# The end of a fused attention and mixture-of-experts kernel: roots in smaller slots, two adds on GpSimd, the last batch centred before it is scaled

## The chip, the cores and the metric

One NeuronCore of a Trainium2 chip runs the kernel. The metric is the device time of one execution in microseconds (us). Engines are named as the profile names them: PE is TensorE's matmul side, DVE is VectorE, ACT is ScalarE, POOL is GpSimd, SP is SyncE, and SPq is SP's queue of issued transfers.

## The reference, cut to what matters

Eight batches of 512 tokens with 128 features go through two residual blocks. The first is a small recurrence between two linear layers, the second a top-2 mixture of eight experts. Each block's result is normalised over the features and then added to its input:

```
x = x + _layernorm(_L0_attn_ref(_layernorm(x, axis=-1), ...), axis=-1)
x = x + _layernorm(_L0_ffn_ref(_layernorm(x, axis=-1), ...), axis=-1)
```

with `_layernorm(x) = (x - mean(x)) / sqrt(var(x) + eps)`. The change touches only the last line's outer normalisation and its add, for batches 3, 4, 5 and 7. All is float32.

## The kernel before, in words

Tokens lie on the 128 partitions. A batch has G = 4 groups of 128 tokens, so a batch of x or of sums is a tile of 128 partitions by 512 columns, and one token group is 128 by 128.

The expert stage takes 71 tiles of up to 128 (token, expert) pairs, one per slot of a software pipeline. PE does the three layers (L1593, L1630), ACT writes a tile's weighted result to SBUF (`take_y`, L618), and POOL scatters it to the table `pair_rows` in HBM with an indirect transfer four slots later in program order (`send_y`, L446). In slot t POOL sends tile t - 4. As soon as all tiles of a batch have been sent, SP loads the batch's pairs back (L342 for whole batches; L348 for the two halves of batch 7, which need the last tile).

For each batch DVE then adds the two expert results of a token (`sum_pairs`, L1267; `sum_half`, L1279), takes the statistics (`bn_stats`, L1273 and L1284) and aggregates them to mean and variance (L1291). POOL turns variances to 1/sd (`one_over_sd`: an add of eps at L465, a power of -0.5 at L469), and DVE makes -mean/sd of it (`offset`, L1297). The tuple SD_GROUPS says which batches go together: (0,1), (2,3), (4,5), 6, and 7, the last of which takes ACT's square root (`root_last`, L644) and DVE's reciprocal (L1312) instead of POOL's power. ACT scales and shifts batches 0 to 4 and the first half of 7 (`normalise4`, L636; `normalise_last`, L650). DVE does 5, 6 and the second half of 7 (L1305). DVE adds the result to x for every batch (`add`, L1315, one instruction of 128x512; `add_last`, L1327, two of 128x256).

The order on each engine is written out by hand. DVE after the pipeline: normalise 5, add 5, add 2, offset of 6, normalise 6, add 6, add 3, add 4, the two halves of 7 with their statistics, then 7's root, scaling and add. POOL after the pipeline: only 1/sd of batch 6. SP issues its transfers in one fixed order, each behind its wait. Its end is this:

```
            load_half(0)
            load_half(1)
            sp.wait_ge(s_half_in[1], 16)
            sp.wait_ge(d["out"], 5)
            write_out(3)
            sp.wait_ge(d["out"], 6)
            write_out(1)
            sp.wait_ge(d["out"], 7)
            write_out(2)
            sp.wait_ge(d["out_end"], 1)
            write_half(1)
            sp.wait_ge(d["out_end"], 2)
            write_half(0)
```

`write_out(g)` writes GROUPS[g] of x: group 3 is batch 6 (256 KB), group 1 is batches 2 and 3, group 2 is batches 4 and 5 (512 KB each). A half of batch 7 has 128 KB. `d["out"]` counts DVE's adds in their order on DVE, so that 5 means that batch 6 is added.

Of the kernel before, what the change touches and what calls it, by code (L numbers as in the profile page):

```python
# [13 lines left out]
P = 128  # L14
# [3 lines left out]
G = S // P  # L18
# [35 lines left out]
ROOT2, ROOT3 = 3, 3  # L54

GROUPS = ((0, 2), (2, 4), (4, 6), (6, 7), (7, 8))
SD_GROUPS = ((0, 2), (2, 4), (4, 6), (6, 7), (7, 8))


def sandwich_kernel(nc, x_in, w_in_in, b_in_in, w_out_in, b_out_in, decay_in, mix_in,  # L60
                    gate_in, w0_in, w1_in, wo_in, out):
    ctx = ExitStack()
    with ctx:
# [122 lines left out]
        def half_of_pairs(b, k):  # L186
            return pairs_in[b].rearrange("p (j k d) -> p j k d", k=K, d=D)[:, :, k, :]
# [43 lines left out]
        s_rows_in = [sem(f"tile_in{n}") for n in range(RING)]  # L231
        s_y_sent = [sem(f"y_sent{n}") for n in range(Y_SLOTS)]

        names_d = "out_end m stats mv sd rs nm normed normed_here normed_end out x1"
        d = {n: sem("d_" + n) for n in names_d.split()}
        s_pairs_in = [sem(f"pairs_in{n}") for n in range(len(GROUPS))]
        s_half_in = [sem(f"half_in{n}") for n in range(2)]
# [24 lines left out]
        def sums(n):  # L262

            return half_of_pairs(n // G, 0)[:, n % G, :]
# [15 lines left out]
        def _(sp):  # L280
# [91 lines left out]
            sp.wait_ge(s_half_in[1], 16)  # L372
            sp.wait_ge(d["out"], 5)
            write_out(3)
            sp.wait_ge(d["out"], 6)
            write_out(1)
            sp.wait_ge(d["out"], 7)
            write_out(2)
            sp.wait_ge(d["out_end"], 1)
            write_half(1)  # L380
# [5 lines left out]
        def _(pool):  # L386
# [76 lines left out]
            def one_over_sd(g, first, end):  # L463
                pool.wait_ge(d["mv"], end)
                pool.tensor_tensor(  # L465
                    sd4[:, first * G:end * G], mv4[:, first * G:end * G, 1],
                    eps[:].broadcast_to([P, (end - first) * G]), ALU.add).then_inc(d["sd"], 1)
                pool.wait_ge(d["sd"], g + 1)
                pool.tensor_tensor(  # L469
                    rs4[:, first * G:end * G], sd4[:, first * G:end * G],  # L470
                    minus_half[:].broadcast_to([P, (end - first) * G]),
                    ALU.pow).then_inc(d["rs"], 1)
# [6 lines left out]
            for k, s, t in slots():  # L479
                if t == STEP + 1:  # L480
                    rest_power()
                a_slot(k, s)
                send_y(t - 4)
                if t == FIRST_OLD_TILES + 9:
                    one_over_sd(0, *SD_GROUPS[0])
                elif t == FIRST_OLD_TILES + 11:
                    one_over_sd(1, *SD_GROUPS[1])
                elif t == FIRST_OLD_TILES + 13:
                    one_over_sd(2, *SD_GROUPS[2])

            one_over_sd(3, *SD_GROUPS[3])

        @block.scalar
        def _(act):
# [149 lines left out]
                act.activation(sd4[:, last], mv4[:, last, 1], ACT.Sqrt,  # L644
                               bias=eps[:]).then_inc(d["sd"], 1)

            def normalise_last():
                act.wait_ge(d["nm"], len(SD_GROUPS))
                for n in range((B - 1) * G, (B - 1) * G + G // 2):
                    last = act.activation(sums(n), sums(n), ACT.Identity,  # L650
                                          scale=rs4[:, n:n + 1], bias=nm4[:, n:n + 1])
                last.then_inc(d["normed_end"], 1)


            root(1, 0, mv1, sd1)
            normalise1(0, 0, G)
# [54 lines left out]
            normalise4(2, 4, 0, G)  # L711
            act.activation(unused[:], eps[:], ACT.Sqrt)
            root_last()
            normalise_last()

        @block.vector
        def _(dve):
# [552 lines left out]
            def stats_of(b):  # L1270
                dve.wait_ge(d["m"], b + 1)
                for n in range(b * G, (b + 1) * G):
                    last = dve.bn_stats(stats4[:, n, :], sums(n))  # L1273
                last.then_inc(d["stats"], 1)
# [13 lines left out]
            def aggregate(b):  # L1288
                dve.wait_ge(d["stats"], b + 1)
                for n in range(b * G, (b + 1) * G):  # L1290
                    last = dve.bn_aggr(mv4[:, n, :], stats4[:, n, :])  # L1291
                last.then_inc(d["mv"], 1)

            def offset(g):
                first, end = SD_GROUPS[g]
                dve.wait_ge(d["rs"], g + 1)
                dve.scalar_tensor_tensor(out=nm4[:, first * G:end * G],  # L1297
                                         in0=mv4[:, first * G:end * G, 0], scalar=-1.0,
                                         in1=rs4[:, first * G:end * G], op0=ALU.mult,
                                         op1=ALU.mult).then_inc(d["nm"], 1)  # L1300

            def normalise4(g, b, first, end):
                dve.wait_ge(d["nm"], g + 1)
                for n in range(b * G + first, b * G + end):
                    last = dve.tensor_scalar(sums(n), sums(n), rs4[:, n:n + 1], nm4[:, n:n + 1],  # L1305
                                             ALU.mult, ALU.add)
                last.then_inc(d["normed_here"], 1)

            def one_over_last():
                last = slice((B - 1) * G, B * G)  # L1310
                dve.wait_ge(d["sd"], len(SD_GROUPS))
                dve.reciprocal(rs4[:, last], sd4[:, last]).then_inc(d["rs"], 1)  # L1312
# [5 lines left out]
            def add_normed(b):  # L1318
                dve.wait_ge(d["normed"], b + 1)
                add(b)  # L1320

            def add_here(b):
                dve.wait_ge(d["normed_here"], b - 4)
                add(b)

            def add_last(j):
                return dve.tensor_tensor(  # L1327
                    x[:, (B - 1) * G + j:(B - 1) * G + j + 2],
                    x[:, (B - 1) * G + j:(B - 1) * G + j + 2],
                    half_of_pairs(B - 1, 0)[:, j:j + 2], ALU.add)  # L1330

            def table_start(p):
                full_tiles(p)
# [72 lines left out]
            for k, s, t in slots():  # L1406
                if t == 2:
                    table_start(1)
                elif t == 3:
                    table_end(1)  # L1410
                elif t == 4:
                    use_tiles(1)
                    table_start(2)
                elif t == 5:
                    table_end(2)
                elif t == 6:
                    use_tiles(2)
                if k in ROUNDS:
                    a_slot(k, s, 0)
                chunk_of(t + 1)  # L1420
                times_gate_curve(t - 1)
                fetch_w1(t + 1)
                pairs_of_tiles(t)
                if k in ROUNDS:
                    a_slot(k, s, 1)
                if t == STEP - 2:
                    rest_sums(0, G)
                elif t == STEP - 1:
                    rest_sums(G, 2 * G)
                elif t == STEP:  # L1430
                    rest_mean_var()
                elif t == STEP + 4:
                    rest_offset()
                if FULL_TILES - 5 <= t < FULL_TILES - 5 + B:
                    add_nm2(t - (FULL_TILES - 5))
                if t == FIRST_OLD_TILES + 6:
                    sum_pairs(0, 0)
                    stats_of(0)
                elif t == FIRST_OLD_TILES + 7:
                    aggregate(0)  # L1440
                    sum_pairs(0, 1)
                    stats_of(1)
                elif t == FIRST_OLD_TILES + 8:
                    aggregate(1)
                    sum_pairs(1, 2)
                    stats_of(2)
                elif t == FIRST_OLD_TILES + 9:
                    aggregate(2)
                    sum_pairs(1, 3)
                    stats_of(3)  # L1450
                elif t == FIRST_OLD_TILES + 10:
                    offset(0)
                    aggregate(3)
                    sum_pairs(2, 4)
                    stats_of(4)
                elif t == FIRST_OLD_TILES + 11:
                    aggregate(4)
                    sum_pairs(2, 5)
                    stats_of(5)
                elif t == FIRST_OLD_TILES + 12:  # L1460
                    offset(1)
                    aggregate(5)
                elif t == FIRST_OLD_TILES + 13:
                    sum_pairs(3, 6)
                    stats_of(6)
                elif t == FIRST_OLD_TILES + 14:
                    offset(2)
                    aggregate(6)
                elif t == FIRST_OLD_TILES + 15:
                    add_normed(0)  # L1470
                elif t == FIRST_OLD_TILES + 16:
                    add_normed(1)

            normalise4(2, 5, 0, G)
            add_here(5)
            add_normed(2)
            offset(3)
            normalise4(3, 6, 0, G)
            add_here(6)
            add_normed(3)  # L1480
            add_normed(4)
            sum_half(0)
            stats_of_half(0)
            sum_half(1)
            stats_of_half(1)
            aggregate(7)
            one_over_last()
            offset(4)
            normalise4(4, 7, G // 2, G)
            dve.wait_ge(d["normed_here"], 3)  # L1490
            add_last(G // 2).then_inc(d["out_end"], 1)
            dve.wait_ge(d["normed_end"], 1)
            add_last(0).then_inc(d["out_end"], 1)

        @block.tensor
        def _(pe):
# [207 lines left out]
```

## Time and profile before

| | |
|---|---|
| Time, median of 3 runs | 299.33 us |
| Runs | 299.3 to 300.03 us |
| Span of the profiled execution | 297.5 us |
| The profiled execution's own time | not listed apart; the median less the span is 1.8 us |
| PE busy | 254.9 us (86%) |
| DVE busy | 209.0 us (70%) |
| ACT busy | 176.1 us (59%) |
| POOL busy | 164.7 us (55%) |
| Mean granted TensorE clock | 0.925 |

The span runs from the first to the last instruction. Busy shares are means over the whole program. Only the last 15 us or so matter for this change, and there PE has no work from 282.8 us on.

### The profile page before, as it was taken

The numbers are of one execution on the slowest core, as the hardware profiler recorded it, in microseconds if no ns is written. First come the engines' busy times: TensorE is split into PE (matmuls) and PEld (weight loads), VectorE is DVE, ScalarE is ACT, GpSimd is POOL, SyncE is SP. The second block draws the span as 40 slices with busy tenths as digits, with TensorE's granted clock in tenths as the row PEclk, the third lists the DMA queues.
The fourth block names the chain that finished last, engine by engine and source line by source line (L and its number), as shares of the span: only waits on it lengthen the run. The fifth ranks groups of instructions, "written<-read, shape, count | busy, mean of one in ns | idle before, by whom it ended". The sixth has DMA issues, their size and how long they took to land.

```text
span 297.5 us, 8014 instructions
## 1 busy us (share of the span) xinstructions
PE 254.9 (86%) x2056; PEld 235.2 (79%) x2056; DVE 209.0 (70%) x939; ACT 176.1 (59%) x439; POOL 164.7 (55%) x187
## 2 busy tenths in 40 slices
PE   0667696899988899999999999999999999999900
PEld 0226353799987899899979998999999999999900
DVE  3786989786884587658766956787664444798875
ACT  3634358475665676766674565656566566567681
POOL 8000377784188747874776577577533333247840
PEclk9965559599999999999999999999999999999985
DMA  5899711312310132112212211333333114802047
GB/s 144 181 384 316 209 56 48 81 55 67 74 37 30 52 79 62 45 55 76 64 36 75 75 46 47 98 104 90 92 77 90 43 55 134 334 20 81 19 141 212
DMA packets 28139, 29.65 MB, mean 100 GB/s; under 512 B 4570, under 2 KB 21180, under 8 KB 28096
## 3 DMA queue, kind: packets, MB, share of 16 engines
q1 hardware_dynamic: 22832, 20.04, 23.7%
q0 software_dynamic: 4544, 8.97, 9.4%
q8 instruction: 19, 0.31, 0.5%
q10 hardware_dynamic: 720, 0.13, 0.3%
q14 instruction: 24, 0.20, 0.2%
HBM read 17.53 MB, written 12.05 MB: 99 GB/s over the span
## 4 chain that ended last, share of the span: by engine, by line
PE 54%; DVE 16%; POOL 10%; issue 8%; ACT 7%; DVEq 2%; DMA 1%; ACTq 1%; POOLq 0%
PE bank L1593 28%; PE bank L1630 14%; POOL expert_rows L433 5%; PE bank L1528 3%; PE bank L1544 3%; PE bank L1537 2%; DVE sb_w_now L1236 2%; PE bank L1588 2%; POOL pair_rows L446 2%; POOL sb_rs L414 1%; DVE sb_early L824 1%; DVEq L1230 1%; DMA sb_x<-in_L_attn_x 1%; ACT sb_row L546 1%; ACT sb_early L518 1%
## 5 line engine op out<-in xcount | busy, mean ns | idle before, releaser
L1593 PE MATMUL bank<-sb_xeT,sb_w_now 128*128 128x128 f32 x1136 | 140.9, 277 | 1.9 <-DVE sb_gated L1217 1.9
L1593 PEld LDWEIGHTS bank<-sb_xeT,sb_w_now 128*128 128x128 f32 x1136 | 134.6, 194 | 3.6 <-issue 3.6
L446 POOL DMA_INDIRECT pair_rows<-sb_y_rows,sb_y_pair x71 | 71.3, 1004 | 55.4 <-ACT sb_y_rows L618 38.2
L433 POOL DMA_INDIRECT expert_rows<-sb_row,sb_place x64 | 65.0, 1016 | 47.9 <-DVE sb_place L931 29.0
L1217 DVE TENSOR_TENSOR sb_gated<-bank,sb_silu 128x512 f32<-128x512 f32 x71 | 49.0, 689 | 50.9 <-PE bank L1593 35.7
L1630 PE MATMUL bank<-sb_w_raw,sb_gated 128*128 x568 | 76.2, 277 | 2.2 <-ACT sb_y_rows L618 1.4
L1630 PEld LDWEIGHTS bank<-sb_w_raw,sb_gated 128*128 128x128 f32 x568 | 69.0, 192 | 3.8 <-issue 3.6
L589 ACT ACTIVATE sb_silu<-bank 128x512 f32<-128x512 f32 x71 | 42.5, 598 | 18.0 <-PE bank L1593 15.7
L584 ACT ACTIVATE sb_xeT<-bank 128x128 f32<-128x128 f32 x71 | 19.6, 277 | 56.1 <-PE bank L1588 56.0
L607 ACT ACTIVATE sb_w_now<-sb_w_raw 128x512 f32 x71 | 44.4, 625 | 0.4 <-issue 0.4
L1236 DVE COPY sb_w_now<-sb_w_raw 128x512 f32 x71 | 32.3, 455 | 1.5 <-issue 1.5
L618 ACT ACTIVATE sb_y_rows<-bank,sb_y_weight 128x128 f32<-128x128 f32 x71 | 25.8, 364 | 11.0 <-DVE sb_y_weight L1262 9.1
L1588 PE MATMUL bank<-sb_ident,sb_taken_rows 128*128 128x128 f32 x71 | 19.9, 280 | 0.9 <-DMA sb_taken_rows<-expert_rows 0.9
L546 ACT ACTIVATE sb_row<-sb_x,sb_nm,sb_rs 128x128 f32<-128x128 f32 x32 | 13.7, 485 | 5.1 <-DVE sb_nm L780 5.0
L1528 PEld LDWEIGHTS bank<-sb_w_outT,sb_early 128*128 128x128 f32 x64 | 9.7, 226 | 7.8 <-DVE sb_early L824 7.7
L1528 PE MATMUL bank<-sb_w_outT,sb_early 128*128 128x128 f32 x64 | 10.7, 319 | 5.9 <-DVE sb_early L824 5.9
L1516 PE MATMUL bank<-sb_early,sb_w_inT 128*128 128x512 f32 x16 | 11.1, 783 | 2.5 <-DVE sb_early L816 2.5
L1588 PEld LDWEIGHTS bank<-sb_ident,sb_taken_rows 128*128 128x128 f32 x71 | 10.6, 150 | 2.8 <-DMA sb_taken_rows<-expert_rows 1.0
L1544 PEld LDWEIGHTS bank<-sb_gate,sb_early 128*128 128x128 f32 x64 | 9.4, 226 | 3.1 <-ACT sb_early L553 3.1
L1544 PE MATMUL bank<-sb_gate,sb_early 128*128 128x8 f32 x64 | 9.6, 277 | 2.1 <-ACT sb_early L553 2.1
L411 POOL TENSOR_TENSOR sb_sd<-sb_mv,sb_eps 128x4 f32<-128x4 f32 x10 | 2.1, 208 | 16.6 <-DVE sb_mv L767 16.5
L518 ACT ACTIVATE sb_early<-sb_x,sb_nm,sb_rs 128x128 f32<-128x128 f32 x24 | 10.1, 482 | 2.0 <-DVE sb_nm L780 2.0
(179 smaller groups left out, 276.3 us busy)
## 6 DMA issues: line engine op xcount, KB each, us to landing
sb_taken_rows<-expert_rows SPq DMA_DIRECT2D x71, 65.5 KB, 1.9
sb_w_raw<-in_L_ffn_w SPq DMA_DIRECT2D x2, 2048.0 KB, 14.7
sb_pairs_early<-pair_rows SPq DMA_DIRECT2D x3, 1024.0 KB, 7.2
out_dram<-sb_x SPq DMA_DIRECT2D x3, 512.0 KB, 3.8
pair_rows<-sb_y_rows,sb_y_pair POOLq DMA_INDIRECT x71, 2.3
sb_x<-in_L_attn_x SPq DMA_DIRECT2D x4, 256.0 KB, 5.9
expert_rows<-sb_row,sb_place POOLq DMA_INDIRECT x64, 2.5
expert_rows<-sb_pad_row SPq DMA_DIRECT2D x8, 65.5 KB
```

The source lines that it names most:

```text
L433: pool.indirect_dma_start(expert_rows[:, :], bass.IndirectOffsetOnAxis(ap=place[b % ROWS][:, k, j:j + 1], axis=0), row[b % ROWS][:, j, :], ...
L446: pool.indirect_dma_start(pair_rows[:, :], bass.IndirectOffsetOnAxis(ap=y_pair[group % 2][:, t % PAIRS:t % PAIRS + 1], axis=0), y_rows[slo ...
L589: act.activation(silu[t % 2][:], p_l1[:], ACT.Silu).then_inc(c["silu"], 1)
L607: act.activation(w0_now[t % 2][:].rearrange("p (c f) -> p c f", f=D), w_raw_chunks[:, bass.ds(chunks[t], FC), :], ACT.Copy).then_inc(c["w0 ...
L618: act.activation(y_rows[t % Y_SLOTS][:], p_y[t % 2][:, 0:D], ACT.Copy, scale=y_weight[group % 2][:, t % PAIRS:t % PAIRS + 1]).then_inc(c[" ...
L1217: dve.tensor_tensor(gated[t % 2][:], p_l2[:], silu[t % 2][:], ALU.mult).then_inc(c["gated"], 1)
L1236: dve.tensor_copy(w1_now[t % 2][:].rearrange("p (c f) -> p c f", f=D), w_raw_chunks[:, bass.ds(chunks[t] + W_CHUNKS, FC), :]).then_inc(c[" ...
L1528: last = pe.matmul(p_first(b)[:, j * D:(j + 1) * D], states[b % 2][:, j * P:(j + 1) * P], w_outT[:], start=False, stop=(j == G - 1))
L1544: last = pe.matmul(p_second(b)[:, j * E:(j + 1) * E], xn2T[b % 2][:, j * P:(j + 1) * P], gate[:], start=True, stop=True)
L1588: pe.transpose(p_xeT[:, 0:P], taken_rows[:, t % RING, 0:D], ident[:]).then_inc(c["xeT_ps"], 1)
L1593: last = pe.matmul(to[:, n * P:(n + 1) * P], w[:, n * P:(n + 1) * P], x, start=True, stop=True)
L1630: last = pe.matmul(p_y[t % 2][:, 0:D], gated[t % 2][:, n * P:(n + 1) * P], wo.rearrange("p o d -> p (o d)"), start=(n == 0), stop=(n == FC ...
```

## The change

It does five things. (1) SD_GROUPS has six entries: POOL takes batch 4's roots in slot FIRST_OLD_TILES + 12 and batch 5's in slot + 13, where it took both in slot + 13. (2) DVE's offsets of batches 4 and 5 are two instructions, in slots + 13 and + 14, instead of one in slot + 14. (3) The adds to x of batches 3 and 4 go from DVE to POOL, behind the power of batch 6, and SP waits for them by a semaphore of their own, `added`. (4) For batch 7 the mean is subtracted while ACT takes the root: two groups on POOL in one 128x256 instruction, two on DVE. (5) The last step of batch 7 is then, for each group, one DVE instruction x = sums * (1/sd) + x, four in all. `normalise_last` on ACT, the last offset, the last `normalise4` and the 128x256 adds on DVE are gone.

```diff
-SD_GROUPS = ((0, 2), (2, 4), (4, 6), (6, 7), (7, 8))
+SD_GROUPS = ((0, 2), (2, 4), (4, 5), (5, 6), (6, 7), (7, 8))
...
@@ sync
             write_out(3)
-            sp.wait_ge(d["out"], 6)
+            sp.wait_ge(d["added"], 1)
             write_out(1)
-            sp.wait_ge(d["out"], 7)
+            sp.wait_ge(d["added"], 2)
             write_out(2)
...
@@ gpsimd
                     one_over_sd(1, *SD_GROUPS[1])
+                elif t == FIRST_OLD_TILES + 12:
+                    one_over_sd(2, *SD_GROUPS[2])
                 elif t == FIRST_OLD_TILES + 13:
-                    one_over_sd(2, *SD_GROUPS[2])
-
-            one_over_sd(3, *SD_GROUPS[3])
+                    one_over_sd(3, *SD_GROUPS[3])
+
+            one_over_sd(4, *SD_GROUPS[4])
+            for b in (3, 4):
+                pool.wait_ge(d["normed"], b + 1)
+                pool.tensor_tensor(x[:, b * G:(b + 1) * G], x[:, b * G:(b + 1) * G],
+                                   half_of_pairs(b, 0), ALU.add).then_inc(d["added"], 1)
+            pool.wait_ge(d["mv"], B)
+            first = (B - 1) * G
+            pool.tensor_tensor(half_of_pairs(B - 1, 0)[:, 0:2], half_of_pairs(B - 1, 0)[:, 0:2],
+                               mv4[:, first:first + 2, 0:1].broadcast_to([P, 2, D]),
+                               ALU.subtract).then_inc(d["centred"], 1)
...
@@ scalar
-            normalise_last()
...
@@ vector
+            def centre_last():
+                for n in range(B * G - 2, B * G):
+                    last = dve.tensor_scalar(sums(n), sums(n), mv4[:, n, 0:1], None,
+                                             ALU.subtract)
+                last.then_inc(d["centred_here"], 1)
+
             def add_last(j):
-                return dve.tensor_tensor(
-                    x[:, (B - 1) * G + j:(B - 1) * G + j + 2],
-                    x[:, (B - 1) * G + j:(B - 1) * G + j + 2],
-                    half_of_pairs(B - 1, 0)[:, j:j + 2], ALU.add)
+                for n in range((B - 1) * G + j, (B - 1) * G + j + 2):
+                    last = dve.scalar_tensor_tensor(
+                        out=x[:, n, :], in0=sums(n), scalar=rs4[:, n:n + 1], in1=x[:, n, :],
+                        op0=ALU.mult, op1=ALU.add)
+                last.then_inc(d["out_end"], 1)
...
                     stats_of(6)
+                    offset(2)
                 elif t == FIRST_OLD_TILES + 14:
-                    offset(2)
+                    offset(3)
                     aggregate(6)
...
-            normalise4(2, 5, 0, G)
+            normalise4(3, 5, 0, G)
             add_here(5)
             add_normed(2)
-            offset(3)
-            normalise4(3, 6, 0, G)
+            offset(4)
+            normalise4(4, 6, 0, G)
             add_here(6)
-            add_normed(3)
-            add_normed(4)
             sum_half(0)
             stats_of_half(0)
             sum_half(1)
             stats_of_half(1)
             aggregate(7)
+            wait_apart(dve, d["mv"], B)
+            centre_last()
             one_over_last()
-            offset(4)
-            normalise4(4, 7, G // 2, G)
-            dve.wait_ge(d["normed_here"], 3)
-            add_last(G // 2).then_inc(d["out_end"], 1)
-            dve.wait_ge(d["normed_end"], 1)
-            add_last(0).then_inc(d["out_end"], 1)
+            dve.wait_ge(d["rs"], len(SD_GROUPS))
+            dve.wait_ge(d["centred_here"], 1)
+            add_last(G // 2)
+            dve.wait_ge(d["centred"], 1)
+            add_last(0)
```

## Rows read from the trace of the kernel before

**Rows 1.** Chain that ended last, in order of time, from 282 us: start, us, what

```profile
284.62 0.98 POOL pair_rows L446
...
286.98 0.17 DVE sb_nm L1297
...
288.32 1.90 DVE sb_x L1315 x3
```

**Rows 2.** Timeline of SP's queue: start us, us, engine, line, operation

```profile
286.85 0.81 SPq L348 DMA_DIRECT2D sb_early<-pair_rows  x2
290.07 1.66 SPq L353 DMA_DIRECT2D out_dram<-sb_x  x3
294.20 0.90 SPq L358 DMA_DIRECT2D out_dram<-sb_x  x2
```

**Rows 3.** Stretches at the end: us, busy by engine, PEclk, DMA share, GB/s

```profile
290.50:291.00 0.50, 0.00 (x0) 0.00 (x0) 0.47 (x4) 0.00 (x0) 0.00 (x0) 0.50 0.00 1
291.00:291.50 0.50, 0.00 (x0) 0.00 (x0) 0.47 (x3) 0.00 (x0) 0.00 (x0) 0.50 0.90 245
...
296.50:297.00 0.50, 0.00 (x0) 0.00 (x0) 0.00 (x0) 0.00 (x0) 0.00 (x0) 0.50 0.13 36
```

**Rows 4.** Waits of SP's queue from 281 us on: us in total, times, longest

```profile
SPq L353 <- DMA sb_early<-pair_rows: 1.0, 1, 1.0
```

**Rows 5.** Timeline of POOL: a scatter at 106 us, then the last slots

```profile
106.31 0.98 POOL L446 DMA_INDIRECT pair_rows<-sb_y_rows,sb_y_pair  x1 [0.30 <-issue]
...
270.98 1.68 POOL L469 TENSOR_TENSOR sb_rs<-sb_sd,sb_minus_half 128x8 f32<-128x8 f32 x1
...
275.30 0.99 POOL L446 DMA_INDIRECT pair_rows<-sb_y_rows,sb_y_pair  x1 [1.41 <-ACT sb_y_rows L618]
...
276.66 2.00 POOL L469 TENSOR_TENSOR sb_rs<-sb_sd,sb_minus_half 128x8 f32<-128x8 f32 x1
...
281.55 1.40 POOL L446 DMA_INDIRECT pair_rows<-sb_y_rows,sb_y_pair  x1 [0.37 <-issue]
```

**Rows 6.** Timeline of ACT: two results of expert tiles, then batches 2 to 4

```profile
274.09 0.36 ACT L618 ACTIVATE sb_y_rows<-bank,sb_y_weight 128x128 f32<-128x128 f32 x1
280.34 0.36 ACT L618 ACTIVATE sb_y_rows<-bank,sb_y_weight 128x128 f32<-128x128 f32 x1
283.11 4.71 ACT L636 ACTIVATE sb_pairs_early<-sb_pairs_early,sb_nm,sb_rs 128x128 f32<-128x128 f32 x12
```

**Rows 7.** Timeline of POOL: what it executes on 128 columns and on one

```profile
1.08 0.21 POOL L389 MEMSET sb_ones_f<- 128x128 f32 x1
1.83 0.29 POOL L393 TENSOR_SCALAR_AFFINE_SELECT sb_ident<-sb_ident 128x128 f32<-128x128 f32 x1 [0.24 <-POOL sb_pad_row L391]
2.33 0.09 POOL L397 MEMSET sb_pad_row<- 128x1 f32 x1
```

**Rows 8.** Timeline of DVE at the same times as some of POOL's instructions

```profile
106.86 0.68 DVE L1236 COPY sb_w_now<-sb_w_raw 128x512 f32 x1
...
276.45 0.68 DVE L1267 TENSOR_TENSOR sb_early<-sb_early 128x512 f32<-128x512 f32 x1
...
281.41 1.28 DVE L1315 TENSOR_TENSOR sb_x<-sb_x,sb_pairs_early 128x512 f32<-128x512 f32 x2
```

**Rows 9.** Lines L1236 and L469 over the whole span: ns min/median/max, forms

```profile
L1236 DVE COPY sb_w_now<-sb_w_raw x71: 410/417/714, 55.1 to 275.9; 128x512 f32 x71
...
L469 POOL TENSOR_TENSOR sb_rs<-sb_sd,sb_minus_half x4: 1033/1671/2003, 266.3 to 285.9; 128x8 f32<-128x8 f32 x3, 128x4 f32<-128x4 f32 x1
```

**Rows 10.** Timeline of DVE from batch 6's scaling to the last add

```profile
287.18 1.11 DVE L1305 TENSOR_SCALAR sb_early<-sb_early,sb_rs,sb_nm 128x128 f32<-128x128 f32 x4
288.32 0.69 DVE L1315 TENSOR_TENSOR sb_x<-sb_x,sb_early 128x512 f32<-128x512 f32 x1
291.95 0.38 DVE L1291 BATCH_NORM_AGGREGATE sb_mv<-sb_stats 128x2 f32<-128x6 f32 x4
293.74 0.76 DVE L1327 TENSOR_TENSOR sb_x<-sb_x,sb_early 128x256 f32<-128x256 f32 x2
```

More of the change, by code:

```diff
@@ L232, in sandwich_kernel @@
         s_y_sent = [sem(f"y_sent{n}") for n in range(Y_SLOTS)]
-        names_d = "out_end m stats mv sd rs nm normed normed_here normed_end out x1"
+        names_d = "out_end m stats mv sd rs nm normed normed_here centred centred_here out added x1"
         d = {n: sem("d_" + n) for n in names_d.split()}
@@ L645, in root_last @@
                                bias=eps[:]).then_inc(d["sd"], 1)
[L647 to L652, printed above, removed]
             root(1, 0, mv1, sd1)
```

## The prediction

> **What bounds the kernel now.** I read the chain that ended last, then SP's queue, then the stretches of the last microseconds, because the chain alone misleads here. The chain [rows 1] goes from POOL's last scatter (ends 285.60 us) over the power of batch 6 into DVE and stays there: offset, normalise, three adds, the half batches, the last scaling. Read so, every DVE instruction behind 287 us is on the path, and taking adds off DVE should pay in full.
>
> SP's queue and the stretches tell another end. SP issues three output writes from 290.07 us and the two halves from 294.20 [rows 2]. The DMA engines move nothing until about 291.0, are then 0.90 to 1.05 busy in every half microsecond at some 286 GB/s, and run dry just behind 296.5 [rows 3]. These are 256 + 512 + 512 + 128 + 128 = 1,536 KB, one unbroken stream of some 5.45 us. The end of the kernel is therefore: first write issued (290.07), about 1.05 us to its first data, 5.45 us of stream, about 0.95 us to the last instruction = 297.5. DVE's last add ends at 294.50 [rows 10], and the data of the halves merely join the stream. The first 1,280 KB last until 291.1 + 4.55 = 295.65, so a half issued by 294.6 leaves no gap. The actual issues, 294.20 and 294.65 for the second (which has the first half's 0.45 us more), just make it. An earlier last add therefore gains nothing.
>
> What holds the first write? SP's last wait ahead of it is 1.0 us for the second half of batch 7 to land [rows 4]. DVE's add of batch 6, which it waits for too, ends at 289.01 [rows 10], so it has 1.05 us of slack. Beyond that it delays the stream one for one.
>
> **The change, part by part.** *Powers in two slots.* The 8-column power takes 2.00 us here, the 4-column one 1.03 [rows 5, 9]. In slot + 12 POOL has a hole: its send of tile 64 ends at 273.89 and the next starts at 275.30, 0.85 us behind ACT's result of 274.45 [rows 5, 6]. Batch 4's add and power (about 0.25 + 1.1 us) fit it, all but 0.2 us. Slot + 13 then has a power about a microsecond shorter, and tiles 66 and 67 go out 0.6 us earlier. But tile 68's send, at 281.55, stands at 280.70 + 0.85, the same distance from its own ACT result [rows 5, 6]: it was no longer held by the backlog. From there on POOL's chain is the same, so the last scatter and the load of the halves stay. Gain 0; if tile 68's 1.40 us fell to the usual 0.98, at most 0.4.
>
> *Offsets in two.* One DVE instruction more of 0.17 us [rows 1], in slots where DVE waits for PE: 0.
>
> *Two adds leave DVE.* They are two of the three that the chain shows with 1.90 us together, so 1.2 to 1.3 us [rows 1]. DVE would be free at 289.01. The halves land between 289.6 and 290.04, so the statistics start about 0.4 us earlier. By the above this buys nothing, since the stream sets the end.
>
> *Two adds on POOL.* ACT has batch 3 ready by about 286.3 and batch 4 at 287.82 [rows 6], POOL ends the power of batch 6 just ahead of the offset that waits for it, at 286.98 [rows 1]. So the first add starts at 287.0, just when DVE begins its offset, normalise and add of batch 6. The trace has no POOL add of 512 columns. A one-input select of 128 columns takes 0.29 us against 0.09 for one column [rows 7], which is 1.55 ns a column, 0.88 us for 512. With a second input read after the first at the memset's 0.9 ns a column it is 1.34. The ends I keep are 0.69 (DVE's own add, rows 10) and 1.7 (the select's slope twice); I take 1.1, between 0.88 and 1.34. The Trainium skill, "GPSIMD Engine Reference", section 3.1, gives 4,497 ns for an fp32 add of 2,048 columns, a quarter of which is an estimate of 1.12 us.
>
> SP needs these adds only for its second and third write, so their own length is covered up to about 290.5 and 292.8. What matters is whom they hold up. The trace shows DVE and POOL excluding each other. POOL's power at 276.66 took 2.00 us where the median is 1.67, and a DVE add with two SBUF inputs ran until 277.13 [rows 5, 8, 9]. The scatter at 281.55 took 1.40 where another took 0.98, under two DVE adds from 281.41, and it did get in between them: two adds last until 282.69, which would have cost it more [rows 5, 8]. The other way, DVE's 128x512 copy at 106.86 took 0.68 us where the median is 0.417, beside the second half of that other scatter [rows 5, 8, 9]. POOL's instructions so far touch SBUF only briefly; an add of 512 columns does so for nearly its whole length.
>
> So I sum with a full hold of 1.05 us for each add. DVE's offset has the port until 287.15. POOL's add of batch 3: 287.15 to 288.20. DVE's first scaling until 288.5. POOL's add of batch 4 until 289.55. DVE's other three scalings (0.28 each) until 290.4, then the add of batch 6, 0.69, to 291.1. That is 2.1 us later than before, of which 1.05 is slack: the first write goes out 1.05 us later. The Trainium skill, "SBUF — State Buffer", section "Who interferes with whom", has the same rule (a GpSimd instruction that reads SBUF and a Vector one with two SBUF inputs, or in a 2-port mode, lock each other out for the whole instruction); by it the sum is this one, and without it the change costs 0.
>
> *Centring and the last step.* Before, from the end of aggregation (292.33) to the last add 2.17 us [rows 10]. After: two subtractions at 0.28 to 0.34, the reciprocal 0.2, four scale-and-adds. None of these is in the trace; half of a 128x256 add is 0.21, and one of 128x128 with its fixed part is some 0.30. That makes 0.6 + 0.2 + 1.2 = 2.0 us. POOL's subtraction of 256 columns (0.4 to 0.9, I take 0.6) meets DVE's two, and can add its 0.6: 2.0 to 2.6. With the add of batch 6 at 291.1 the aggregation ends at 293.3, the halves are issued by 295.4 and 295.9. The delayed stream's first 1,280 KB last until 296.7, so they still join it without a gap. Cost 0.
>
> **Sum:** +1.05 us on 297.5, so 298.5 us of span. The runs' median lies 1.83 us above this profile's span, and I add the difference to the median: 300.4 us.
>
> **The rivals.** A measurement of this kernel can tell about 0.3%, 0.9 us.
>
> *A, forecast (0.50).* Both adds on POOL get in ahead of DVE's add of batch 6. With holds of 0.7 to 1.6 us the cost is 0.35 to 2.15: 299.7 to 301.5, mostly over 300.2.
>
> *B, DVE keeps the port (0.18).* Only one POOL add gets in; the other runs behind the add of batch 6, which ends at 290.05. The stream starts on time, but the first half's sum waits until 291.15, the aggregation ends at 293.3, the halves go out at about 294.8 to 295.4 and 295.4 to 296.0, and the stream has a gap. End +0.35 to +0.95: 300.0. For it: DVE's instructions follow each other without a pause. Against it: the scatter that got in between two adds.
>
> *C, no hold (0.22).* POOL's add touches the port in small pieces, DVE loses a few tenths, which the 1.05 us of slack cover: 299.3, no difference. For it: POOL's power at 270.98 took its usual 1.68 us [rows 5] with DVE at work beside it; but it reads 8 columns. It decides below a loss of 1.05 us on DVE for both adds together.
>
> *D, the other side (0.10).* The end is set by the last half's fixed time from issue to landing, not by the bytes. Then the DVE work taken away pays: 0.4 us earlier statistics, a tail shorter by 0.15, and up to 0.4 from the last scatters: 298.4 to 298.8. Against it: the unbroken busy share in rows 3. It would need gaps between the last writes.
>
> **How the numbers follow.** The likeliest case gives 300.4. Its own range is 299.7 to 301.5. Eight in ten: below, C and part of D, 298.9; above, A with a hold of 1.45 us, 301.2. Slower by over 0.3% is most of A and a little of B: 0.49. Within 0.3%: the rest of A, B, C and part of D: 0.42. Faster by over 0.3%: 0.09, the far end of D.
>
> **What would show it.** Right: two POOL adds of 1.0 to 1.3 us between 287.0 and 289.7; a gap or long instructions in DVE between 287.0 and 291; SP's first write near 291.1 instead of 290.07; the DMA stream unbroken and as long as before; the last scatter still near 284.6. Wrong: the first write still at 290.07 with the adds done beside DVE (C), a hole in the DMA share before the halves (B), a last landing that moves earlier with the last add (D), or a last scatter before 284.3.

## The result, and the profile after

The changed kernel takes 301.32 us (median; 301.22 to 301.4), the kernel before 299.31 us: a ratio of 1.0067, 95% interval 1.0047 to 1.0087. So it is slower by 2.0 us, where +1.05 was forecast (300.4, range 298.9 to 301.2). The span of the profiled execution went from 297.5 to 299.6 us.

DVE's timeline of the changed kernel from batch 6's offset on, the counterpart of [rows 10]:

```profile
287.20 1.23 DVE L1300 SCALAR_TENSOR_TENSOR sb_nm<-sb_mv,sb_rs 128x4 f32<-128x4 f32 x1 [1.52 <-POOL sb_rs L469]
288.47 2.02 DVE L1308 TENSOR_SCALAR sb_early<-sb_early,sb_rs,sb_nm 128x128 f32<-128x128 f32 x4
290.52 0.69 DVE L1318 TENSOR_TENSOR sb_x<-sb_x,sb_early 128x512 f32<-128x512 f32 x1
...
292.95 0.38 DVE L1294 BATCH_NORM_AGGREGATE sb_mv<-sb_stats 128x2 f32<-128x6 f32 x4
293.48 0.82 DVE L1331 TENSOR_SCALAR sb_early<-sb_early,sb_mv 128x128 f32<-128x128 f32 x2
...
294.42 1.14 DVE L1337 SCALAR_TENSOR_TENSOR sb_x<-sb_early,sb_rs,sb_x 128x128 f32<-128x128 f32 x4
```

POOL's timeline of the same kernel:

```profile
284.84 0.98 POOL L446 DMA_INDIRECT pair_rows<-sb_y_rows,sb_y_pair  x1 [0.30 <-issue]
...
287.16 2.47 POOL L496 TENSOR_TENSOR sb_x<-sb_x,sb_pairs_early 128x512 f32<-128x512 f32 x2
293.41 0.61 POOL L500 TENSOR_TENSOR sb_early<-sb_early,sb_mv 128x256 f32<-128x256 f32 x1 [3.78 <-DVE sb_mv L1294]
```

An offset of four columns took 1.23 us where it took 0.17, and the four scalings 2.02 where they took 1.11: DVE stood 1.06 + 0.91 = 1.97 us behind POOL's two adds of 1.24 us. Nothing in these two rows is marked as a wait for POOL's adds. The lost time is inside the durations.

SP's queue, the counterpart of [rows 2], then its waits ([rows 4]):

```profile
291.30 1.66 SPq L353 DMA_DIRECT2D out_dram<-sb_x  x3
295.06 1.23 SPq L358 DMA_DIRECT2D out_dram<-sb_x  x2
```

```profile
SPq L373 <- DVE sb_x L1318: 3.3, 1, 3.3
...
SPq L63 <- DMA out_dram<-sb_x: 2.0, 1, 2.0
SPq L63 <- PEq L63: 1.1, 1, 1.1
```

The first write went out 1.23 us later, and now it waits for DVE's add of batch 6 instead of for the halves. The stream behind it is as before:

```profile
292.00:292.50 0.50, 0.00 (x0) 0.00 (x0) 0.47 (x3) 0.00 (x0) 0.00 (x0) 0.50 0.48 144
292.50:293.00 0.50, 0.00 (x0) 0.00 (x0) 0.47 (x3) 0.00 (x0) 0.00 (x0) 0.50 0.99 255
...
297.00:297.50 0.50, 0.00 (x0) 0.00 (x0) 0.00 (x0) 0.00 (x0) 0.00 (x0) 0.50 0.95 283
297.50:298.00 0.50, 0.00 (x0) 0.00 (x0) 0.00 (x0) 0.00 (x0) 0.00 (x0) 0.50 0.56 167
```

It ends about 1.2 us later than in [rows 3]. But the span ends 2.1 us later. The other 0.9 us are in the last wait above: SP, finished with its transfers, waits 1.1 us for the closing barrier. In the kernel before that wait was 0.2 us. The name PEq in it is only the engine that came last by the profile. PE was done at 283. Line 63 (the end of the block, where each engine drains) tells which engine it was. First the changed kernel, then the kernel before; the columns are ns min/median/max and first and last start:

```profile
L63 PEldq DRAIN  x1: 688/688/688, 282.4 to 282.4; - x1
L63 ACTq DRAIN  x1: 328/328/328, 293.4 to 293.4; - x1
L63 POOLq DRAIN  x1: 5975/5975/5975, 293.4 to 293.4; - x1
L63 DVEq DRAIN  x1: 1057/1057/1057, 294.6 to 294.6; - x1
...
L63 SPq DRAIN  x1: 7/7/7, 298.5 to 298.5; - x1
```

```profile
L63 POOLq DRAIN  x1: 6395/6395/6395, 285.9 to 285.9; - x1
...
L63 SPq DRAIN  x1: 7/7/7, 297.3 to 297.3; - x1
```

POOL's drain begins with the issue of its last instruction. Taking that instruction off (0.61 and 1.03 us), it lasts 5.37 us both times. Before, it was over at 292.3, hidden. With the centring on POOL it is over at 299.4, 0.9 us past SP's.

The bill of the profiled executions: 0.22 us that the whole program is late at the last scatter already (284.84 against 284.62; in the traces of all the runs it starts between 283.94 and 284.84), 1.01 for the first write beyond that, 0.88 for the drain. Together 2.1 us.

### The profile page after: what moved, and what is told of

Its sections match the earlier page's. It is cut to its first block, busy times and chain, and to the rows that moved or that the text cites. A ratio compares the mean times of both kernels' runs of the same rounds, so it can differ in the third digit from the quotient of the medians.

```text
span 299.6 us, 8019 instructions
## 1 busy us (share of the span) xinstructions
PE 253.8 (85%) x2056; PEld 234.7 (78%) x2056; DVE 209.9 (70%) x939; ACT 175.0 (58%) x437; POOL 168.5 (56%) x192
## 4 chain that ended last, share of the span: by engine, by line
PE 44%; POOL 17%; DVE 13%; issue 12%; ACT 5%; DMA 4%; DVEq 1%; SPq 1%; ACTq 0%; POOLq 0%
PE bank L1603 24%; PE bank L1640 12%; POOL expert_rows L433 10%; POOL pair_rows L446 3%; DVE sb_w_now L1239 2%; PE bank L1538 2%; DMA pair_rows<-sb_y_rows,sb_y_pair 2%; PE bank L1554 2%; PE bank L1598 2%; POOL sb_rs L414 1%; DMA sb_x<-in_L_attn_x 1%; PE bank L1547 1%; ACT sb_early L529 1%; ACT sb_y_rows L629 1%; ACT sb_silu L600 1%
## 5 line engine op out<-in xcount | busy, mean ns | idle before, releaser
L1526 PE MATMUL bank<-sb_early,sb_w_inT 128*128 128x512 f32 x16 | 10.4, 740 | 2.5 <-DVE sb_early L819 2.5
```

## The experiments

Each was timed in turns with the kernel before on the same chip; ratios are to that. From run to run the kernel before moved between 298.4 and 299.9 us, and the granted TensorE clock moved with it: its 19 runs at a mean of 0.925 to 0.928 took 299.2 to 299.9 us, its eight at 0.953 or 0.954 took 298.4 to 298.75. So a tenth or two of a per cent between two experiments can be the clock. The loss of the change is not: its four runs are at 0.924 to 0.929, and 301.3 us is 1.9 above the median of those 19.

**e1: all centring on DVE, POOL's adds stay.**

```diff
-            pool.wait_ge(d["mv"], B)
...
-                               ALU.subtract).then_inc(d["centred"], 1)
...
-                for n in range(B * G - 2, B * G):
+                for n in range(B * G - G, B * G):
```

> The changed kernel with all four centring subtractions of batch 7 on DVE, so that POOL's last instruction is its second add (ends 289.6). Theory: the change has two prices. POOL's adds hold DVE up, which delays the first output write by 1.2 us, and POOL's drain lasts 5.4 us from its last instruction, which the centring at 293.4 to 294.0 carries to 299.4, 0.9 us past SP's last landing. Without the centring on POOL only the first price is left: first write still near 291.3, POOL's drain over by 295, span 298.7, 300.3 to 300.5 us. Rival: the drain waits for nothing of POOL's own, and the last 0.9 us come from the last half's slower landing: then 301.2 to 301.4 again.

Measured 300.07 us, ratio 1.0022 (1.0009 to 1.0035). Its DVE, then SP's first write and POOL's drain:

```profile
286.97 1.23 DVE L1295 SCALAR_TENSOR_TENSOR sb_nm<-sb_mv,sb_rs 128x4 f32<-128x4 f32 x1 [1.52 <-POOL sb_rs L469]
288.24 2.01 DVE L1303 TENSOR_SCALAR sb_early<-sb_early,sb_rs,sb_nm 128x128 f32<-128x128 f32 x4
```

```profile
291.06 1.66 SPq L353 DMA_DIRECT2D out_dram<-sb_x  x3
```

```profile
L63 POOLq DRAIN  x1: 6873/6873/6873, 287.9 to 287.9; - x1
```

The last scatter here starts at 284.62, as before the change, and the first write is 0.99 us later than in [rows 2]. That is the adds' price without the shift. Span 298.4. The drain, over at 294.8, costs nothing. The time is 0.2 us below what I expected; three of its six runs had a clock of 0.947 to 0.952, and the profiled one, at 0.933, took 300.18.

**e2: adds of batches 3 and 4 back on DVE, POOL centres** (SP waits for `d["out"]` 6 and 7 again).

```diff
-            for b in (3, 4):
-                pool.wait_ge(d["normed"], b + 1)
...
             add_here(6)
+            add_normed(3)
+            add_normed(4)
```

> The changed kernel with the adds of batches 3 and 4 back on DVE; POOL still centres half of batch 7. Theory: DVE is not held up, batch 6's offset takes 0.17 us and its four scalings 1.1 again, the first write goes out near 290.2. POOL's centring ends near 293.2 and its drain near 298.6, about 1 us past SP's last landing: span 298.7, 300.3 to 300.5 us. Rival (only the first write counts): 299.2 to 299.5.

Measured 300.5 us, ratio 1.0049 (1.0032 to 1.0066). Offset and scalings are back to the old durations and the first write to 290.20, yet the end is late:

```profile
286.82 0.16 DVE L1296 SCALAR_TENSOR_TENSOR sb_nm<-sb_mv,sb_rs 128x4 f32<-128x4 f32 x1 [1.52 <-POOL sb_rs L469]
287.02 1.11 DVE L1304 TENSOR_SCALAR sb_early<-sb_early,sb_rs,sb_nm 128x128 f32<-128x128 f32 x4
```

```profile
L63 POOLq DRAIN  x1: 5973/5973/5973, 292.2 to 292.2; - x1
...
L63 SPq DRAIN  x1: 7/7/7, 297.4 to 297.4; - x1
```

POOL's drain ends at 298.2, 0.8 us behind SP's, and the span is 298.4. Each half of the change that is on POOL has a price of its own.

**e3: the kernel before with one dead memset on POOL behind the last add.**

```diff
+        late = sb("late", [P, 1])
...
             one_over_sd(3, *SD_GROUPS[3])
+            pool.wait_ge(d["out_end"], 2)
+            pool.memset(late[:], 0.0)
```

> The kernel before, with one 128x1 memset of an unused tile added on POOL behind the last add of batch 7 (294.5). Theory (POOL's drain lasts some 5.4 us from POOL's last instruction and holds the final barrier): it ends near 300.0, span 300.1, 301.8 to 302.0 us, although the memset takes 0.1 us and nothing reads it. Rival (the drain only waits for all engines or the last transfers): 299.3.

Measured 302.07 us, ratio 1.009 (1.0073 to 1.0107), 0.1 us above my band.

```profile
294.62 0.10 POOL L494 MEMSET sb_late<- 128x1 f32 x1 [7.63 <-DVE sb_x L1330]
```

```profile
L63 POOLq DRAIN  x1: 5425/5425/5425, 294.6 to 294.6; - x1
...
L63 SPq DRAIN  x1: 7/7/7, 297.4 to 297.4; - x1
```

A tenth of a microsecond of work that nothing reads costs 2.7 us. The drain starts later and keeps its length.

**e6: the same memset behind the aggregation of batch 7** (`pool.wait_ge(d["mv"], B)` in place of the wait above).

> The kernel before with one 128x1 memset of an unused tile on POOL, behind the aggregation of batch 7 (292.35). Theory (the end is the later of SP's last landing and POOL's last instruction plus 5.35 us): drain over near 297.8, 0.5 us behind SP: span 297.9, 299.7 to 299.9 us. Rival (a late POOL instruction costs a fixed 2.7 us, as in e3_late_memset): 302.

Measured 299.77 us, ratio 1.0015 (1.0003 to 1.0026), span 298.0.

```profile
L63 POOLq DRAIN  x1: 5425/5425/5425, 292.3 to 292.3; - x1
...
L63 SPq DRAIN  x1: 7/7/7, 297.1 to 297.1; - x1
```

The end is the later of two, and the price is not fixed: POOL's (297.8) is 0.7 us past SP's (297.1).

**e4: the kernel before with the powers of batches 4 and 5 in two slots.**

```diff
-SD_GROUPS = ((0, 2), (2, 4), (4, 6), (6, 7), (7, 8))
+SD_GROUPS = ((0, 2), (2, 4), (4, 5), (5, 6), (6, 7), (7, 8))
...
+                elif t == FIRST_OLD_TILES + 12:
+                    one_over_sd(2, *SD_GROUPS[2])
...
```

> The kernel before with only the powers of batches 4 and 5 in two slots and their offsets in two instructions. Theory: the last scatter still starts near 284.6 to 284.8, the first write near 290.1 to 290.3, 299.2 to 299.5 us. Rival (the shorter backlog on POOL moves the last scatter): last scatter near 284.2, 298.9.

Measured 298.96 us, ratio 0.9985 (0.9974 to 0.9995), 0.2 us below my band.

```profile
281.34 1.40 POOL L446 DMA_INDIRECT pair_rows<-sb_y_rows,sb_y_pair  x1 [0.90 <-ACT sb_y_rows L620]
```

Tile 68's scatter now sits idle 0.90 us until ACT's result and still takes 1.40, so POOL's backlog was not what held it. But the time is the 298.9 of the rival, and the last scatter, at 284.41, lies between the 284.2 of the rival and the 284.6 of the theory. In the trace the 0.2 us are gone by the first write, which goes out at 290.10, and the profiled span is 297.5, as before. So the trace doesn't show where the small gain in time comes from, the clock doesn't explain it (the runs are below those of the kernel before at the same clock), and e10, which has this part too, does not show it. Its cause stays open.

**e5: e1 with POOL's adds behind DVE's add of batch 6** (one more line on POOL, `pool.wait_ge(d["out"], 5)`).

> The kernel of e1_centre_on_dve (adds of batches 3 and 4 on POOL, no centring there) with POOL's adds waiting for DVE's add of batch 6. Theory: DVE's offset takes 0.16 us and its scalings 1.1 again, the first write goes out at about 290.1 to 290.3 instead of 291.1. POOL's adds then run from 289.0 to 291.5 and hold up DVE's two half sums, so the last add ends near 295 and the halves come 0.5 us too late for an unbroken stream: 299.5 to 299.9 us. Rival (POOL's adds cost DVE nothing wherever they stand, and e1 was late for another reason): first write still near 291.1, 300.1.

Measured 299.39 us, ratio 1.001 (0.9996 to 1.0024), 0.1 us below my band. The profiled execution is 0.33 us early at the last scatter (284.29).

```profile
286.65 0.16 DVE L1296 SCALAR_TENSOR_TENSOR sb_nm<-sb_mv,sb_rs 128x4 f32<-128x4 f32 x1 [1.52 <-POOL sb_rs L468]
...
289.08 1.23 DVE L1278 TENSOR_TENSOR sb_early<-sb_early 128x256 f32<-128x256 f32 x1 [0.39 <-DMA sb_early<-pair_rows]
...
290.75 0.96 DVE L1278 TENSOR_TENSOR sb_early<-sb_early 128x256 f32<-128x256 f32 x1
```

```profile
288.77 2.66 POOL L497 TENSOR_TENSOR sb_x<-sb_x,sb_pairs_early 128x512 f32<-128x512 f32 x2 [2.16 <-DVE sb_x L1314]
```

```profile
L63 POOLq DRAIN  x1: 8023/8023/8023, 288.7 to 288.7; - x1
```

The hold has moved on to the two half sums (1.23 and 0.96 us for 0.42 and 0.41), the first write is at 289.76, as far behind the last scatter as in the kernel before, and only a little is lost. The stream gets no hole, against my expectation. The same adds cost 0.7 us in e1 and 0.1 to 0.3 here. The two intervals overlap, so the times alone don't separate them; the first write, 0.99 us late in e1 and not late here, says that their place decides. POOL's drain is over at 296.7 here, 0.3 us ahead of SP's (297.0). So a last instruction of POOL that ends at 291.4 still costs nothing, and one that ends at 292.5 (e6) does.

**e7: SP's first write no longer waits for the halves to land.**

```diff
-            sp.wait_ge(s_half_in[1], 16)
             sp.wait_ge(d["out"], 5)
```

> The kernel before, SP no longer waiting for the second half of batch 7 to land ahead of its first write. Theory (the stream of writes bounds the end): first write at 289.05 instead of 290.07, behind the loads in the queue, stream up to 1 us earlier; then the last half, issued at 294.6, is bound by its own issue to landing of about 2.0 us instead of 2.4: span 297.0 to 297.2, 298.8 to 299.0 us. Rival (the end is already bound by the last half's issue): 299.3.

Measured 298.93 us, ratio 0.9986 (0.9977 to 0.9995). SP's first write goes out at 288.72. The stream begins earlier and gets a hole ahead of the last half:

```profile
291.00:291.50 0.50, 0.00 (x0) 0.00 (x0) 0.47 (x3) 0.00 (x0) 0.00 (x0) 0.50 0.95 288
...
294.00:294.50 0.50, 0.00 (x0) 0.00 (x0) 0.18 (x1) 0.00 (x0) 0.00 (x0) 0.50 0.58 166
294.50:295.00 0.50, 0.00 (x0) 0.00 (x0) 0.00 (x0) 0.00 (x0) 0.00 (x0) 0.50 0.42 124
295.00:295.50 0.50, 0.00 (x0) 0.00 (x0) 0.00 (x0) 0.00 (x0) 0.00 (x0) 0.50 0.87 244
```

From here the last half's issue bounds the end, and it lands 1.9 us after issue instead of 2.4.

**e8: e4 with the add of batch 3 moved into DVE's idle time, batches 2 and 3 written first, no wait for the halves.**

```diff
-            sp.wait_ge(s_half_in[1], 16)
             sp.wait_ge(d["out"], 5)
-            write_out(3)
-            sp.wait_ge(d["out"], 6)
             write_out(1)
+            sp.wait_ge(d["out"], 6)
+            write_out(3)
...
             add_normed(2)
+            add_normed(3)
             offset(4)
...
-            add_normed(3)
```

> The kernel of e4_split_only, with DVE's add of batch 3 moved into its wait for batch 6's power (285.5 to 287.0) and SP writing batches 2 and 3 first, without waiting for the halves to land. Theory: the output stream starts right behind the loads, near 289.6 instead of 291.1, and DVE reaches the half sums 0.3 to 0.4 us earlier (289.8); the end is then the last half's issue at 294.2 plus 2 us to landing: span 296.6 to 296.9, 298.2 to 298.6 us. Rival (the writes take bandwidth from the loads of the halves, which land later): 299 or more.

Measured 298.07 us, ratio 0.9956 (0.9942 to 0.997), 0.1 us below my band.

```profile
286.14 0.69 DVE L1316 TENSOR_TENSOR sb_x<-sb_x,sb_pairs_early 128x512 f32<-128x512 f32 x1 [0.85 <-ACT sb_pairs_early L637]
286.82 0.16 DVE L1298 SCALAR_TENSOR_TENSOR sb_nm<-sb_mv,sb_rs 128x4 f32<-128x4 f32 x1
```

```profile
287.54 2.69 SPq L353 DMA_DIRECT2D out_dram<-sb_x  x3
293.56 0.89 SPq L358 DMA_DIRECT2D out_dram<-sb_x  x2
```

The add fits exactly into the 1.5 us in which DVE waited for batch 6's power. The loads of the halves take up to 3.2 us to land, against 3.1 in e4, so the rival is not borne out. This version beats both kernels. It changes three things at once, and the runs split its gain only in part: e7 has the wait for the halves alone.

**e9: e8 with the change's last step, centring shared by DVE and ACT.**

```diff
+                last = act.activation(sums(n), sums(n), ACT.Identity,
+                                      bias=nm4[:, n:n + 1])
...
+            minus_mean()
+            centre_last()
             one_over_last()
...
+            add_last(G // 2)
+            dve.wait_ge(d["centred"], 1)
+            add_last(0)
```

> The kernel of e8_stream_early with the change's last step, its centring shared by DVE (second half) and ACT behind the root (first half, bias -mean), nothing on POOL. Theory (in e8 the end is the last half's issue plus 1.9 us, so now the tail counts): from the end of aggregation to the last add 2.0 to 2.1 us instead of 2.17, span 296.1 to 296.3, 297.9 to 298.1 us, at best 0.1 to 0.2 below e8. Rival (the form of the last step pays little, the pointer wait and the negation eat it): equal to e8 or 0.1 above.

Measured 297.57 us, ratio 0.9952 (0.9937 to 0.9967), span 295.8, 0.3 us below my band.

```profile
291.18 0.38 DVE L1292 BATCH_NORM_AGGREGATE sb_mv<-sb_stats 128x2 f32<-128x6 f32 x4
...
291.78 0.48 DVE L1334 TENSOR_SCALAR sb_early<-sb_early,sb_mv 128x128 f32<-128x128 f32 x2
...
292.38 1.14 DVE L1340 SCALAR_TENSOR_TENSOR sb_x<-sb_early,sb_rs,sb_x 128x128 f32<-128x128 f32 x4
```

From the end of aggregation (291.56) to the last add (293.52) it is 1.96 us, against 2.17 before and in e8. The trace shows the 0.2 us. The intervals of e8 and e9 overlap, so the times don't separate them.

**e10: the changed kernel with both POOL parts on DVE** (the edits of e1 and e2 together).

> The changed kernel with both parts that it put on POOL taken back to DVE (adds of batches 3 and 4, and all four centring subtractions); left are the powers in two slots and the new last step. Theory (the two POOL parts are the whole loss): first write near 290.1, POOL's drain over by 292.3, last add near 294.5, stream unbroken: 298.9 to 299.3 us, as e4_split_only. Rival (the new last step has a price of its own): 299.6 or more.

Measured 299.25 us, ratio 1.0009 (0.9998 to 1.002). SP's first write and POOL's drain:

```profile
289.59 1.66 SPq L353 DMA_DIRECT2D out_dram<-sb_x  x3
```

```profile
L63 POOLq DRAIN  x1: 6402/6402/6402, 285.2 to 285.2; - x1
```

The last scatter starts at 283.94 here, 0.7 us earlier than before. Counted from it, the first write is 0.2 us later than before and not 1.0 as in e1; the drain is over at 291.6. What is left of the change, the slots and the new last step, makes no difference to the kernel before beyond 0.2%. The two parts on POOL are the loss. The interval lies just above that of e4, so a price of the new last step of about 0.2% isn't excluded by the times. The traces show none: from the last scatter to the end of the span it is 13.1 us in both.

## Why the prediction was wrong in size, point by point

*What bounds the kernel.* "The end of the kernel is therefore: first write issued (290.07), about 1.05 us to its first data, 5.45 us of stream, about 0.95 us to the last instruction" was right for the kernel before and incomplete for the change. It is one of two ends. The other, POOL's last instruction plus 5.37 us, was in the trace of the kernel before as a drain of 6.4 us over at 292.3, and I did not look for it. The row of line 63 shown above was there to be read.

*Powers and offsets in more slots.* Tile 68's scatter still waits for ACT, as forecast, and takes its 1.40 us. The last scatter of e4 is 0.2 us earlier, within the movement between traces, and the span is the same. Right at 0 in the trace; the 0.15% that e4's times gain are not explained.

*The two adds leaving DVE.* No run takes them off DVE without giving POOL the hold. e5 comes nearest, and with the adds off DVE it is no faster than e10, which has them there (299.39 and 299.25 us). That fits a gain of 0 and doesn't prove it. Where the stream has a hole, earlier arithmetic pays: in e8 the last add ends 9.40 us after the last scatter started and the span 11.84, in e7 9.89 and 12.31.

*The two adds on POOL.* I took 1.1 us for each and measured 1.24. I forecast 2.1 us on DVE and measured 1.97; a first write 1.05 us later and measured 1.01 (after taking off the shift) and 0.99 (e1). One detail was wrong. I let the offset go first and hold up the scalings twice. In fact POOL's add started 0.04 us ahead of the offset (287.16 and 287.20), so the offset of four columns bore a full hold. The sum is the same. The Trainium skill, "SBUF — State Buffer", section "Who interferes with whom", says that whoever issues first keeps the shared pair for the whole instruction; the trace agrees, with 1.23 us for a 0.17 us instruction.

*Centring and the last step.* The failed step is "Cost 0." I priced POOL's subtraction by what it does to DVE: 0.6 us expected, 0.61 measured, and it does hold DVE's two subtractions (0.82 us against 0.48 in e9). From the end of aggregation to the last add it was 2.23 us, within the 2.0 to 2.6 forecast, and the halves still joined the stream. I left out what a late instruction on POOL does to the end. That term measured +0.88 us in the profile. Alone it costs 0.5% (e2), and e3 and e6 show that it follows the time of POOL's last instruction and nothing that the instruction does.

*The rivals.* A was right in its mechanism. That 301.32 also lies in its range of 299.7 to 301.5 is luck: the two adds alone give 300.07 (e1). B's mechanism, a POOL add behind the add of batch 6, did not happen, and forced for both adds in e5 it cost 0.1 to 0.3 us, below the 0.35 to 0.95 I gave it. C fell with the 1.23 us. D fell in the kernel before (unbroken stream), and e7 and e8 show the point from which it holds: once the stream has a hole, the last half's issue counts.

*The range.* With the drain in it, the forecast's own terms give this: aggregation over at 293.3, POOL's subtraction 0.6, drain 5.37, and the 0.2 us that the span of the kernel before still lasts behind the later drain, together 299.5 us of span. That is 0.9 to 1.0 above the forecast's 298.5, so 301.3 to 301.4 us against 301.32 measured. That it meets the median so closely is partly luck: runs of one kernel differ by more than that, and the last scatter of the profiled execution was 0.22 us late.

## What to carry to other kernels

Look for the end of the program on every engine, not only on the one with the last transfer: take the drain rows at the end and ask, for each engine, how late its last instruction may be. Work moved to POOL "beside" DVE is not free: here POOL's adds and its subtraction held up DVE's offset (1.23 us for 0.17), its half sums (1.23 for 0.42), its scalings (2.02 for 1.11) and its subtractions (0.82 for 0.48). Of DVE's work beside them only the statistics kept their time (0.49 us in e5). Look first for a place where DVE idles. And where an output stream bounds the end, look for a write that can be issued earlier before making the arithmetic in front of the last one faster: the first gained 0.14% in e7, the new last step nothing in e10 and 0.2 us in the trace of e9.

## What the runs showed of the hardware that was not expected

POOL's drain at the end of this program lasts 5.3 to 5.4 us from the end of POOL's last instruction, whether that is a power (before), an add (e1), a subtraction (after, e2) or a one-column memset (e3, e6). What it consists of, and whether it is there without scatters, was not tried; all these kernels send 71 + 64 scatters through POOL.

A hold by POOL shows on DVE as duration, not as idle time, and also hits the smallest instruction (1.23 us for 0.17). DVE's two statistics at 290.35 us in e5 lie wholly beside POOL's adds and take the usual 0.49.

The write stream ran at some 340 GB/s in e8 and 330 in e9, which has the same order of writes, against some 290 in the other kernels. Two stretches of e8, with the DMA share well over 1:

```profile
290.50:291.00 0.50, 0.00 (x0) 0.00 (x0) 0.47 (x2) 0.00 (x0) 0.00 (x0) 0.50 1.14 345
291.00:291.50 0.50, 0.00 (x0) 0.00 (x0) 0.47 (x5) 0.00 (x0) 0.00 (x0) 0.50 1.15 346
```

That the first write is queued behind loads that still move is not enough: so it is in e7 (288.72 us, DMA share 0.99 in that half microsecond), and its stream runs at some 290, as its row above shows. e8 and e9 issue their first write earlier still (287.54 and 287.41), when the loads have hardly begun to move data, and begin with 512 KB where e7 begins with 256. Which of the two makes the stream faster was not tried and stays open.
